# Down products of two MLP stages in plain fp32, without a split of hidden layer and weights

## What is computed

```
x_norm2 = layer_norm(x) * (1 + scale_m) + shift_m
h = gelu(x_norm2 @ W_mlp1 + b_mlp1)        # 128 -> 512
h = h @ W_mlp2 + b_mlp2                    # 512 -> 128, the down product
x = x + gate_m * h
```

## Time and profile before

| | us |
|---|---|
| median of 3 runs | 3569.41 |
| lowest, highest | 3560.76, 3570.86 |
| the profiled execution | 3567.66 |
| its span, first to last instruction | 3565.9 |
| TensorE busy (matmuls) | 3088.2 (87%) |
| VectorE busy | 2757.3 (77%) |
| ScalarE busy | 2269.3 (64%) |
| GpSimd busy | 1172.1 (33%) |

### The profile page before, as it was taken

One profiled execution on the slowest core, in us unless ns is written; L12 is line 12 of the kernel. 1 busy time (PEld: TensorE's weight loads), 2 busy tenths in 40 slices (PEclk: granted clock), 3 DMA queues, 4 the chain that ended last, 5 costly groups with the idle time before them and its releaser, 6 DMA issues. The chain is left out here.

```text
span 3565.9 us, 94724 instructions
## 1 busy us (share of the span) xinstructions
PE 3088.2 (87%) x32127; PEld 2065.5 (58%) x32127; DVE 2757.3 (77%) x12477; ACT 2269.3 (64%) x5572; POOL 1172.1 (33%) x1374
## 2 busy tenths in 40 slices
PE   6999877777777769889999997889999998879999
PEld 3454434444444437656666665556666665558887
DVE  5888688999888978588887767868887775956665
ACT  2666567767667657557776665637776665646665
POOL 0000055665555656521122213531112211531221
PEclk9999988888778979999999998989999998979999
DMA  2111000000000000144444430034444441000000
GB/s 84 29 32 30 16 9 8 6 9 8 6 8 8 5 1 1 27 100 108 105 107 102 106 88 3 1 89 104 108 105 100 105 105 28 1 24 10 13 13 16
DMA packets 138900, 162.90 MB, mean 46 GB/s; under 512 B 41206, under 2 KB 88758, under 8 KB 138038
## 3 DMA queue, kind: packets, MB, share of 16 engines
q1 hardware_dynamic: 126262, 130.80, 14.5%
q0 software_dynamic: 12160, 26.04, 3.1%
HBM read 16.33 MB, written 4.19 MB: 6 GB/s over the span
## 5 line engine op out<-in xcount | busy, mean ns | idle before, releaser
L1367 ACT ACTIVATE attn_pT<-attn_t 128x512 f32<-128x512 f32 (+1 forms) x1024 | 556.3, 597 | 318.7 <-PE attn_t L1624 318.5
L1484 DVE TENSOR_REDUCE attn_mx<-attn_s 128x4 f32<-128x512 f32 (+1 forms) x1024 | 549.2, 578 | 136.6 <-PE attn_s L1609 135.4
L1609 PEld LDWEIGHTS attn_s<-packed_keys,packed_queries 32*128 32x128 f32 x4096 | 275.0, 188 | 162.8 <-DVE attn_mx L1484 96.9
L653 ACT ACTIVATE topk_prob<-topk_s,topk_nmx 128x77 f32<-128x77 f32 x1024 | 249.2, 327 | 182.3 <-DVE topk_work L832 156.1
L1282 POOL DMA_DIRECT2D packed_queries<-attn_om x256 | 143.0, 559 | 641.2 <-ACT attn_om L1360 637.3
L498 POOL TENSOR_SCALAR topk_mask<-topk_work 128x308 f32<-128x308 f32 x256 | 250.4, 978 | 314.4 <-DVE topk_work L837 313.3
L1609 PE MATMUL attn_s<-packed_keys,packed_queries 32*128 32x128 f32 (+1 forms) x4096 | 339.7, 286 | 15.4 <-DVE attn_mx L1484 9.1
L1649 PE MATMUL attn_o<-attn_pT,attn_vp 128*18 128x128 f32 (+1 forms) x8192 | 326.2, 277 | 0.0
L1027 PE MATMUL topk_t<-ident,topk_prob 128*77 128x128 f32 x1024 | 186.8, 313 | 138.0 <-POOL topk_prob L502 137.3
L1624 PE MATMUL attn_t<-packed_queries,packed_keys 32*128 32x128 f32 (+1 forms) x4096 | 300.1, 264 | 0.3 <-ACT attn_pT L1367 0.3
L1027 PEld LDWEIGHTS topk_t<-ident,topk_prob 128*77 128x77 f32 x1024 | 141.4, 172 | 242.8 <-issue 150.5
(11 more groups left out here) (316 smaller groups left out, 7859.0 us busy)
## 6 DMA issues: line engine op xcount, KB each, us to landing
packed_queries<-attn_qT SPq DMA_DIRECT2D x720, 64.0 KB, 2.2
packed_keys<-attn_kT SPq DMA_DIRECT2D x384, 64.0 KB, 2.1
packed_queries<-attn_om POOLq DMA_DIRECT2D x256, 64.0 KB, 2.3
packed_queries<-zero_rows SPq DMA_DIRECT2D x120, 128.0 KB, 2.7
packed_keys<-attn_kT SPq DMA_DIRECT2D x384, 39.0 KB, 2.2
kbd<-window_kT SPq DMA_DIRECT2D x512, 8.0 KB
kbd<-topk_kT SPq DMA_DIRECT2D x512, 4.8 KB
weights<-in_weights SPq DMA_DIRECT2D x1, 3267.0 KB, 13.1
```

Of the source, the lines that this page charges most:

```text
L653: last = nc.scalar.activation(prob[:, u % 4, h * keys:(h + 1) * keys], s_ps[:, u % 2, h * keys:(h + 1) * keys], ACT.Exp, scale=SCALE, bias ...
L1367: nc.scalar.activation(pT[0:keys, c % 2, h, :], t_ps[0:keys, h, :], ACT.Exp, scale=SCALE).then_inc(s_exp, 1)
L1484: nc.vector.tensor_reduce(mx[:, (c // 2) % 2, 2 * k + h, :], sc, AX.X, ALU.max).then_inc(s_max, 1)
L1609: last = nc.tensor.matmul(s_ps[:, h, k * KW:(k + 1) * KW], r.qp[32 * j:32 * j + 32, buf, k, b * T:(b + 1) * T], r.kp[32 * j:32 * j + 32, b ...
```

## The change

In layers 1 and 2 the hidden chunk is no longer split: the casts at L1936, the subtractions at L1863 and L1942 and the tile `hid2` go, and so do the split weights `w2` and the wait for them. The down product is one plain fp32 matmul per chunk, of the weights as they lie in SBUF by `hid` as gelu wrote it. It waits for gelu's `s_hid`. Gelu waits, before it writes `hid` again, for the down product of four chunks before. Layer 0 stays as it is, and so do the up products.

```diff
-        w1, w2 = sb("w1", [C, 2, W1], F32R), sb("w2", [C, 2, NC * C], F32R)
+        w1 = sb("w1", [C, 2, W1], F32R)
+        w2 = sb("w2", [C, 2, NC * C], F32R) if swiglu else None
...
-        hid2 = sb("hid2", [C, NC, 2, GT], F32R)
+        hid2 = sb("hid2", [C, NC, 2, GT], F32R) if swiglu else None
...
-                    if swiglu or c < NC - 1:
+                    if swiglu:
                         pool.wait_ge(s_hi, n + 1)
...
-                split_weights(nc, nc.vector.tensor_copy, dve, w2, r.W(name, 0, NC * C), s_w, 2)
+                if swiglu:
+                    split_weights(nc, nc.vector.tensor_copy, dve, w2, r.W(name, 0, NC * C), s_w, 2)
...
-                    if not swiglu:
-                        after(dve, s_down, n - 3)
-                        dve.wait_ge(s_hid, n + 1)
-                        nc.vector.tensor_copy(hid2[:, c, 0, :], hid[:, c % NB, :]).then_inc(s_hi, 1)
                     if c == 2 and nxt2:
                         ln_apply(g + 2)
-                    if c == 3 and not swiglu:
-                        dve.wait_ge(s_hi, n + 1)
-                        after(dve, s_lo, n)
-                        nc.vector.tensor_tensor(hid2[:, c, 1, :], hid[:, c % NB, :], hid2[:, c, 0, :].bitcast(F32),
-                                                ALU.subtract).then_inc(s_lo, 1)
...
                     if work and not swiglu:
-                        after(act, s_lo, n - 3)
+                        after(act, s_down, n - 3)
...
                     after(pe, s_pg, g - 1)
-                    pe.wait_ge(s_w, 4)
+                    if swiglu:
+                        pe.wait_ge(s_w, 4)
+                if not swiglu:
+                    pe.wait_ge(s_hid, n + 1)
+                    nc.tensor.matmul(y_ps[:, par, :], r.W(name, c * C), hid[:, c % NB, :],
+                                     start=(c == 0), stop=(c == NC - 1)).then_inc(s_down, 1)
+                    return
                 pe.wait_ge(s_lo, n + 1)
```

## The result

| | median, us | runs | ratio to the kernel before | 95% interval |
|---|---|---|---|---|
| kernel before, beside it | 3570.1 | 4 | | |
| changed kernel | 3523.8 | 4 | 0.9882 | 0.9869 to 0.9895 |
| changed kernel, again | 3525.5 | 6 | 0.9865 | 0.9842 to 0.9888 |
| changed kernel, a third time | 3530.9 | 6 | 0.9879 | 0.9850 to 0.9908 |

What follows compares the result with a forecast made beforehand. VectorE and GpSimd holding each other up were taken to make `xn` late for TensorE in MLP 1 and 2. Per layer 19.8 plus 1.4 gives 21.2, two layers 42.4: 3569.4 - 42.4 = 3527.0 us, range 3514 to 3543.

Steps and rivals of the forecast that it cites:

- step 3: MLP 1 and 2: TensorE needs 7.10 us a group; the loop through `xn` fits with 0.6 to 0.8 us margin.
- step 1: MLP 1 and 2: casts and subtractions removed, `xn` falls from 2.06 to 1.12 us, VectorE keeps 4.3 us a group.
- step 2: TensorE, MLP 1 and 2: a plain fp32 down product takes 0.855 us, 0.155 more each, 0.62 a group.
- The refine row: Profile row of the refine stage: an fp32 512-column product between three-pass products costs 0.853 us, used to price the down product.
- step 4: MLP prologue: the split of the second weights goes, but was hidden behind GpSimd's `rstd`, so it brings 0.
- step 5: Start of the MLP loop: without GpSimd stretching the split of `hT`, TensorE reaches L2001 1.4 us earlier per layer.
- Steady part: Middle of MLP 1 and 2: 13 groups fall from 8.62 to 7.10 us, 19.8 us per layer.
- step 6: End of the MLP loop, 17.53 us: TensorE nearly full already, change between -0.3 and +0.4, taken as 0.
- A: Rival, MLP 1 and 2: `xn` stays stretched, 0.1 to 0.3 us a group, 3530 to 3535 us; chance 0.13.
- B: Rival, MLP 1 and 2: the fp32 product costs 0.945 us, kernel 3538 or 3539 us; chance 0.15.
- C: Rival, MLP 1 and 2: fp32 products drop the clock to 1.2 GHz, kernel about 3700 us; chance 0.03.
- D: Rival, MLP 1 and 2: VectorE's fullness was slack, TensorE's waits set elsewhere; 20 us added, 3589 us; chance 0.03.

Runs made afterwards that it cites:

- the both-kept run: Changed kernel with casts and subtractions of layers 1 and 2 put back into a tile nobody reads, no product waiting for them: 3572.1 us, ratio 1.0013.

## Why the prediction was right, point by point

- **The bound before.** The place was right (VectorE, held up by GpSimd, `xn` late), but "VectorE works all the time" was not quite the mechanism. VectorE waited once in each group, for the transposes at L2041. What closed was a loop: transpose of `xn` (L2001), an up product, **one down product**, transposes (L2041), residual, variance, `rstd`, split of `hT`, the last cast, `xn`, and the transpose again. (`rstd` is ready at 2226.39, long before `xn` starts at 2227.93. It is in the loop because of what stands behind it on GpSimd: the subtraction from 2226.36 to 2227.73, beside which the last cast lasts 1.51 us.) In the earlier trace rows the loop's TensorE part, L2001 to L2041, is 1.86 us and the rest, L2041 to L2001, 6.77. The experiments fix this: with the fp32 product in it (split kept) the first part is 2.03 and the second 6.77, together 8.79 by the distance of the transposes; with two passes at full clock they are 1.63 and 6.76, together 8.39, which is 8.63 less one pass of 0.23. Had VectorE's fullness been the bound, all three would be the same. This is the part of step 3 that I had written for the kernel after and not applied to the one before.
- **The removed work (step 1).** `xn` fell from 2.06 to 1.12 as written. VectorE keeps 4.07 us a group, expected 4.3, the difference being the overlap of records that follow each other.
- **The added work (step 2).** 0.853 measured, 0.855 used. The refine row was the right one because it had the same neighbours. Four times 512 cycles at 2.4 GHz are 0.853 us, so a pass of the plain product costs what its 512 columns take at one a cycle, 0.213, and a split pass, 0.233, costs 0.02 more. That is where my estimate of 0.93 went wrong: the 0.853 agrees with the count of four passes in the Trainium skill (FP8 and Floating Point Precision, "TensorE Precision Notes"); the price of a pass was mine.
- **TensorE's sum and the new loop (step 3).** 7.10 expected, 7.09 measured. The loop from L2041 to the end of `xn` takes 2235.58 - 2231.33 = 4.25 us where TensorE needs 5.10; expected 4.3.
- **Prologue (step 4).** 0 expected. VectorE's idle ahead of `xn` rose from 0.25 to 1.20 us, with `rstd` as releaser, as said. First statistics to first up product took 8.69 us instead of 8.80.
- **Start of the loop (step 5).** 1.4 a layer expected; 1.7 and 1.8 measured (9.85 to 8.11 and 9.83 to 8.01 us).
- **Steady part.** 19.8 a layer expected, 20.4 and 20.6 measured (112.08 to 91.69, 112.11 to 91.51). I priced all 13 distances at 7.10, but the first has no transposes at L2041 and takes 6.66 and 6.62: that is 0.44 and 0.48 of the missing 0.6 and 0.8. The rest is that the others take 7.09 and 7.07.
- **End (step 6).** 0 expected, 0.03 and 0.01 measured.
- **Sum.** 42.4 expected, 44.9 in the two stages. The remaining 1.4 of the profiled difference and the 0.7 by which the median of before rose with a fourth run are scatter.
- **The rivals.** A and B did not happen, nor C; D is refuted by the group of 7.09 us and by the both-kept run. My last sign, that I am wrong if another stage changes by more than a few us, was drawn too tight: attention 1 came out 5.2 us longer, and with the same code it varies by 21. But the mechanism of C, a lower granted clock, turned out to be near on the other side: it hits not the changed kernel, which fills TensorE, but the versions with two passes and with the subtractions alone, which leave it idle.

## What to carry to other kernels

A wait on the engine that is fullest in the program can come from a loop through another engine; follow the loop once round and add up both parts before calling either engine the bound, for then each pass in the loop has its price. Work that is off the path on GpSimd is free only where it meets no VectorE instruction that it blocks: look at what GpSimd's in-order queue releases at the same moment. And a more costly product on TensorE can be the better one, if what it spares is a preparation on the engines that hold the loop.

## What the runs showed of the hardware

- **Less TensorE work, slower kernel.** Taking four passes (0.93 us) out of a group of 8.64 us lowered the granted clock of the stretch from 1.00 to 0.87 and raised the group to 9.7 to 10.0 us in nine of thirteen. No single gap in the time line was longer than 1.63 us. The same passes in groups of 6.36 us kept 1.00.
- **Blocking adds up, one VectorE instruction for each GpSimd instruction.** `xn`, four VectorE instructions of together 1.12 us, took 2.06 us beside one GpSimd subtraction (the other engine's 1.3 us grew by at most 0.1) and 3.93 us beside three in a row, which together took 3.73. In the first case one of the four was stretched, to 1.29 us, in the second three.
- **A plain fp32 product of 512 columns** costs 0.853 us among fp32r passes, change of kind included; three fp32r passes cost 0.70. Exactness costs 0.155 us on TensorE, not the third more that the pass count suggests.
